# Graph layers on one core: the later layers spread over 29 slots, four graphs to a loop body

## The reference

```
hi = x @ W1[:H];  hj = x @ W1[H:]                       # block 0, for every pair (i, j) of nodes
y  = layernorm(relu(hi[i] + hj[j] + b1) @ W2 + b2) * gamma + beta
x  = layernorm(x + sum_j adj[i, j] * y[i, j])
x  = layernorm(x + relu((D^-1/2 adj D^-1/2 x) W^T + b))  # block 1
x  = layernorm(x + mask * (relu(((1 + eps) x + adj^T x) W1 + b1) W2 + b2))   # block 2
h  = x; three times: h = relu(layernorm(adj^T (h Ws[i]) + bs[i] + h) * g + beta)   # block 3
out = layernorm(x + h)
```

## Time and profile before

| what | value |
|---|---|
| median of 3 runs | 3404.64 us |
| profiled execution | 3402.17 us |
| its span | 3400.4 us |
| TensorE busy | 2933.5 us (86%) |
| VectorE busy | 2919.2 us (86%) |
| ScalarE busy | 2821.7 us (83%) |
| GpSimd busy | 403.7 us (12%) |
| mean granted TensorE clock | 0.945 |
| y products, L369 | 4096 instructions, 2152.3 us busy |
| weighted sums, L624 | 8192 instructions, 1953.1 us busy |
| hidden units on ScalarE, L507 | 1429.6 + 219.4 us busy |
| squares, L517 | 1024 instructions, 1164.1 us busy |

### The profile page before, as it was taken

How to read it: one execution, slowest core, us unless ns; L and a number is a source line. 1 busy time by engine, 2 the same in 40 slices (tenths; PEclk the granted TensorE clock), 3 DMA queues, 4 the chain that set the end, 5 groups by cost and what they waited for, 6 DMA issues and landing times.

```text
span 3400.4 us, 69689 instructions
## 1 busy us (share of the span) xinstructions
PE 2933.5 (86%) x10882; PEld 1150.1 (34%) x10882; DVE 2919.2 (86%) x21905; ACT 2821.7 (83%) x7620; POOL 403.7 (12%) x978
## 2 busy tenths in 40 slices
PE   8988888888888888888888888888888888888894
PEld 2333333333333333333333333333333333333332
DVE  5988888888888888888888888888888888888896
ACT  8988888888888888888888888888888888888892
POOL 0111111111111111111111111111111111111111
PEclk9999999999999999999999999999999999999996
DMA  3544444444444444444444344444444444434442
GB/s 123 208 159 174 182 167 156 169 191 162 158 171 183 169 156 159 196 167 158 158 181 184 156 159 185 179 159 157 175 190 156 159 175 183 164 156 167 192 162 106
DMA packets 170182, 570.56 MB, mean 168 GB/s; under 512 B 68608, under 2 KB 104320, under 8 KB 104320
## 3 DMA queue, kind: packets, MB, share of 16 engines
q1 hardware_dynamic: 169856, 567.82, 42.8%
HBM read 555.17 MB, written 8.39 MB: 166 GB/s over the span
## 4 chain that ended last, share of the span: by engine, by line
DVE 29%; PE 24%; issue 17%; ACT 14%; SPq 5%; DMA 5%; POOL 4%; DVEq 1%; ACTq 0%; POOLq 0%
PE y_ps L369 14%; DVE h L624 13%; ACT h L507 8%; PE ss_ps L381 6%; DVE h L610 5%; DMA devs<-dev_rows 5%; SPq L286 5%; POOL rs L850 3%; ACT sq L517 2%; DVE gT L624 2%; PE prod_bank L432 2%; ACT dev_rows L524 2%; DVE stats L648 2%; ACT h L555 1%; DVE x L657 1%
## 5 line engine op out<-in xcount | busy, mean ns | idle before, releaser
L369 PE MATMUL y_ps<-h,w2c 128*128 128x512 f32 x4096 | 2152.3, 637 | 209.7 <-DVE h L610 207.1
L624 DVE CUSTOM_DVE_ANT_0 h<-h,cb 128x128 f32<-128x128 f32 x8192 | 1953.1, 283 | 9.4 <-DMA cb<-c_scratch 0.4
L507 ACT ACTIVATE h<-uv_ps,uT 128x128 f32<-128x128 f32 x4928 | 1429.6, 400 | 235.5 <-DVE gT L624 230.3
L517 ACT ACTIVATE sq<-y_ps,b2c_col 128x1024 f32<-128x1024 f32 x1024 | 1164.1, 1137 | 143.8 <-PE y_ps L369 134.9
L369 PEld LDWEIGHTS y_ps<-h,w2c 128*128 128x128 f32 x4096 | 694.7, 196 | 1091.2 <-issue 934.0
L610 DVE TENSOR_SCALAR h<-vT,uT 128x128 f32<-128x128 f32 x2560 | 591.8, 282 | 188.6 <-issue 158.8
L624 DVE DVE_READ_ACCUMULATOR2_ANT gT<- 128x1 f32 x8192 | 670.8, 82 | 0.1
L381 PE MATMUL ss_ps<-sq,sel 128*32 128x512 f32 x4096 | 581.4, 642 | 0.5 <-ACT sq L517 0.5
L848 POOL TENSOR_TENSOR var_eps<-mv,eps_col 128x1 f32<-128x1 f32 x448 | 84.8, 189 | 2657.3 <-DVE mv L651 2657.3
L850 POOL TENSOR_TENSOR rs<-var_eps,minus_half 128x1 f32<-128x1 f32 x448 | 277.0, 618 | 35.1
L507 ACT ACTIVATE h<-vT,uT 128x128 f32<-128x128 f32 x704 | 219.4, 400 | 0.0
(11 more groups left out here) (99 smaller groups left out, 1556.2 us busy)
## 6 DMA issues: line engine op xcount, KB each, us to landing
cb<-c_scratch SPq DMA_DIRECT2D x512, 1024.0 KB, 8.1
adj_c<-in_adj_dram SPq DMA_DIRECT2D x512, 8.0 KB
devs<-dev_rows SPq DMA_DIRECT2D x512, 8.0 KB
x_in<-in_x_dram SPq DMA_DIRECT2D x64, 64.0 KB, 9.5
c_scratch<-c SPq DMA_DIRECT2D x128, 32.0 KB, 1.4
adj_in<-in_adj_dram SPq DMA_DIRECT2D x64, 64.0 KB, 2.0
x_res<-in_x_dram SPq DMA_DIRECT2D x64, 64.0 KB, 1.9
out_dram<-x SPq DMA_DIRECT2D x64, 64.0 KB, 10.1
```

Of the source, the lines that this page charges most:

```text
L369: op = pe.matmul(y_ps[:, t % 2, c0:c0 + COLS], w2c[:], h[:, t, c0:c0 + COLS], start=True, stop=True)
L507: op = act.activation(h[:, t, n * P:(n + 1) * P], v, ACT.Relu, bias=uT[:, i:i + 1])
L517: act.activation(sq[:, t % SQ_RING, :], y_ps[:, t % 2, :], ACT.Square, bias=b2c_col[:], scale=float(P) ** -0.5).then_inc(sq_done, 1)
L624: op = dve.tensor_tensor_reduce(h[:, t, cols], h[:, t, cols], cb[:, t // 2, c0:c0 + P], 1.0, 0.0, ALU.mult, ALU.add, gT[:, i:i + 1])
```

## The change

The later layers get a table of their own length, 29 slots, and start at lag 32 (28 after START), a whole number of iterations, so that in each iteration the graph two back is at slot s and the graph three back at slot s + 16. All buffers of the later layers get a second copy, picked by the parity b of the graph, and each parity has its own PSUM bank for prod, the turned adjacency and the coefficients' sum. uT and vT get a second copy too; turning x and making u and v are moved to slots 1 to 3 of the same graph. The weighted sums lag 14 slots behind START, not 15. VectorE makes two hidden units in each slot. A norm is applied seven places after its first step (before: four, and five for the affine of block 3). The loop body holds four graphs. SP loads for the later layers ahead of the output's store.

```
-TTR_LAG = START + 15
-TAIL_LAG = START + 29
+TTR_LAG = START + 14
+TAIL_LAG = START + 28
+UNROLL = 4
+SPLIT_AT = 13
-NORM_AT, AFFINE_AT = 4, 5
+NORM_AT = 7
-def vector_units(t):
-    return 3 if t % 2 == 0 else 2
+VECTOR_UNITS = 2
...
-    ("g_keep", 2, 0), ("l0_mm", 2, 2), ("l0_sum", 2, 5), ("ln0", 2, 6), ("x1_scaled", 3, 3),
-    ("l1_agg", 3, 4), ("l1_agg_keep", 3, 8), ("l1_mm", 4, 2), ("l1_bias", 4, 5), ("l1_relu", 4, 7),
-    ("ln1", 5, 0), ("l2_agg", 5, 4), ("l2_agg_keep", 5, 8),
...
-    ("l3_relu2", 14, 5), ("final_sum", 14, 7), ("ln3", 14, 8),
+    ("g_keep", 2, 0), ("l0_mm", 2, 4), ("l0_sum", 3, 3), ("ln0", 3, 4), ("x1_scaled", 4, 5),
+    ("l1_agg", 5, 0), ("l1_agg_keep", 5, 8), ("l1_mm", 6, 0), ("l1_bias", 6, 7), ("l1_relu", 7, 0),
+    ("ln1", 7, 2), ("l2_agg", 8, 4), ("l2_agg_keep", 9, 2),
+    ("l2_mm1", 9, 4), ("l2_relu", 10, 2), ("l2_mm2", 10, 4), ("l2_sum", 11, 2), ("ln2", 11, 3),
+    ("l3_agg0", 12, 4), ("l3_agg_keep0", 13, 2), ("l3_mm0", 13, 4), ("l3_sum0", 14, 2),
+    ("l3_ln0", 14, 3), ("l3_relu0", 16, 2), ("l3_agg1", 19, 0), ("l3_agg_keep1", 19, 8),
+    ("l3_mm1", 20, 0), ("l3_sum1", 21, 1), ("l3_ln1", 21, 2), ("l3_relu1", 22, 6),
+    ("l3_agg2", 23, 0), ("l3_agg_keep2", 23, 8), ("l3_mm2", 24, 0), ("l3_sum2", 25, 1), ("l3_ln2", 25, 2),
+    ("l3_relu2", 26, 6), ("final_sum", 28, 2), ("ln3", 28, 3),
...
-        prod = prod_bank[:, 0, :]
+        prod_bank = [ps(f"prod_bank{b}", [P, 4, P]) for b in range(2)]
+        xturn_ps, u_ps, v_ps = (uv_ps[:, i, :] for i in range(3))
+        prod = [prod_bank[b][:, 0, :] for b in range(2)]
...
-            for i in range(4):
-                iteration(i + 1, (i, *(i - d if i >= d else None for d in range(1, 4))))
-            with eng.Fori(4, G - 1) as g:
-                iteration(g + 1, (g, g - 1, g - 2, g - 3))
+            first = 4 + (G - 5) % UNROLL
+            for i in range(first):
+                iteration(i + 1, about(i), i % 2)
+            with eng.Fori(0, (G - 1 - first) // UNROLL) as rounds:
+                for n in range(UNROLL):
+                    g = UNROLL * rounds + (first + n)
+                    iteration(g + 1, (g, g - 1, g - 2, g - 3), (first + n) % 2)
...
+        def tails(graphs, buf, s):
+            return [(graphs[d], (buf - d) % 2, (s + SLOTS * (d - 2)) * FINE) for d in (2, 3)]
...
+                    load_tail(old, 1 - buf)                      # SP, now here
+                if oldest is not None:
+                    wait_apart(sp, normed["ln3"], oldest + 1)
...
-                if old is not None:
-                    load_tail(old)                               # SP, was last
...
-                    hidden_step = BLOCK_UNITS if ht == 0 else 0
+                    hidden_step = BLOCK_UNITS if ht == 0 else 0 if t == 0 else 1
...
-                        later_layers(g, place * FINE + k, place * FINE + k + 1)
+                        for g, b, place in tails(graphs, buf, s):
+                            later_layers(g, b, place + k, place + k + 1)
```

More of the change, by code:

```diff
@@ L406, in later_layers @@
                     wait(pe, g_kept, g + 1)
[L407 to L410, removed]
+                    pe.matmul(out, gT_keep[:, b, :], w2cg[:], start=True, stop=False)
+                    pe.matmul(out, adjT[:, b, :], beta0[:], start=False, stop=True).then_inc(l0_made, 1)
                 if due("l1_agg"):
@@ L453, in _ @@
             pe.wait_ge(ident_set, 1)
-            turn_x(0)
             pe.wait_ge(weights_in, 16 * WEIGHTS)
@@ L459, in _, with iteration @@
             pe.wait_ge(set_up, 1)
-            def iteration(after, graphs):
+            def iteration(after, graphs, buf):
                 new = graphs[0]
@@ L465, in iteration @@
                         later_set_up()
-                    g, place = lagging(graphs, s, TAIL_LAG)
                     yg, t = lagging(graphs, s, START + 1)
-                    if s == START - 1 and new is not None:
-                        make_uv(new)
                     if yg is not None:
                         products(yg, t, 0)
-                    if s == 14 and after is not None:
-                        turn_x(after)
-                    later_layers(g, place * FINE, place * FINE + 4)
+                    for g, b, place in tails(graphs, buf, s):
+                        later_layers(g, b, place, place + 4)
                     if yg is not None:
                         products(yg, t, 1)
-                    later_layers(g, place * FINE + 4, (place + 1) * FINE)
+                    for g, b, place in tails(graphs, buf, s):
+                        later_layers(g, b, place + 4, place + FINE)
+                    if s == 1 and new is not None:
+                        turn_x(new)
+                    if s == 2 and new is not None:
+                        make_uv(new)
                     sg, t = lagging(graphs, s, START + 3)
@@ L582, in iteration @@
                         deviations(vg, t // HALF)
-                    later_layers(g, place + 1, place + 4)
-                    first = vector_units(ht)
-                    for n in range(first, DUO_UNITS):
-                        if n == first + 2:
-                            later_layers(g, place + 4, place + 6)
-                        if n == first + 4:
-                            later_layers(g, place + 6, place + 8)
-                        if hg is not None:
-                            hidden(hg, ht, n)
-                    if s == SLOTS - 1 and after is not None:
-                        keep_xT(after)
-                    if s == START - 1 and new is not None:
-                        keep_uv(new)
-                    later_layers(g, place + 8, place + FINE)
+                    if s == START - 1 and new is not None:
+                        keep_uv(new, buf)
+                    tail_steps(1, 4)
+                    for n in range(VECTOR_UNITS, DUO_UNITS):
+                        if n == VECTOR_UNITS + 2:
+                            tail_steps(4, 6)
+                        if n == VECTOR_UNITS + 4:
+                            tail_steps(6, 8)
+                        if hg is not None:
+                            hidden(hg, hb, ht, n)
+                    if s == 1 and new is not None:
+                        keep_xT(new)
+                    tail_steps(8, FINE)
             program(act, iteration)
@@ L601, in _, with hidden @@
         def _(dve):
-            def hidden(g, t, n):
+            def hidden(g, b, t, n):
                 if n == 0:
```

259 lines of the change are left out of this document (130 added, 129 removed), and 5 rows, old and new, of the table AT.

## The result

The changed kernel takes 3016.64 us in the median (3013.08 to 3017.53, four runs) against 3405.36 us for the kernel before timed beside it: ratio 0.8855, 95% interval 0.884 to 0.887. The forecast was 3089 us with a range from 3020 to 3200; the time lies 3.4 us under its lower end. The direction and the two mechanisms came out, the size of the largest term, the period, did not. The profiled execution has a span of 3014.8 us.

The account below looks back on a forecast made before the run. No single engine was taken to bound the kernel, but work order and hand-overs. Start 185, 59 periods of 46.3 (2731.7), branches back 44.2 and end 124.2 gave 3085 us; plus 1.8 and 2.5, 3089 us, range 3020 to 3200.

Parts of the forecast that it names:

- the two mechanisms: Of the 315 us forecast gain, 153 from fewer branches back and some 160 from a shorter period per graph.
- the period: Time per graph inside the loop: 49.07 us falls to 46.3, ScalarE's busy time; floor 45.1 (VectorE), ceiling 47.5.
- The branches back: End of each loop pass: 13 instead of 58, at 3.4 us each, 153 us less; 44 us remain.
- The third rival: VectorE's floor is reached in the loop: period 45.1 us, 3018 us or less; chance 0.16.
- VectorE's waits: Later layers' wider places remove VectorE's 1.4 us for GpSimd power and 1.0 us for TensorE's products per graph.
- The lag: Weighted sums 14 slots behind: ScalarE's 1.0 us wait goes; coefficients lose one slot, with 1.4 us to spare.
- The slower rival: Coefficients reach VectorE's weighted sums too late: up to 7.0 us wait per graph, 3502 us; chance 0.03.
- SP's queue, turn_x and keep_uv: Reordered SP transfers: no gain, no loss; turn_x and keep_uv moved to slots 1 to 3, costed at zero.
- The ends: Outside the steady periods: 185 us up to iteration 4's gT_keep, 124.2 us from iteration 63's copy to the end.
- the drain's 5 us: Last graph's later layers share queues with the graph before: between 0 and 14 us more, taken as 5.
- The first rival: ScalarE takes over and its waits for y_ps and aggregates stay: period 48.7 us, 3231 us; chance 0.11.
- the second: Rival: the loop's stall is per graph, not per branch back, so 45 x 3.4 us returns, 3242 us; chance 0.03.

Follow-up runs that it names:

- experiment 1: The kernel before with only its loop body changed to four graphs (13 branches back, not 58): 3264.16 us, ratio 0.9597.
- experiment 7: The changed kernel with ScalarE reading v from SBUF in all slots (SPLIT_AT 0, not 13): 3167.66 us, ratio 0.9318.
- experiment 4: The changed kernel with VectorE making three and two hidden units in turn, as before the change: 3047.04 us, ratio 0.8961.
- experiment 5: The changed kernel with three and two VectorE units in turn, plus 100 filler memsets shifting the loop in VectorE's stream: 3022.88 us, ratio 0.8876.
- experiment 8: The changed kernel, two runs: ScalarE squaring only half of each y_ps tile, 2949.68 us; VectorE without three of eight units' weighted sums, 3003.89 us.
- experiment 10: The changed kernel with norms applied four places after their first step, not seven: 3117.1 us, ratio 0.9158.
- experiment 9: The changed kernel with weighted sums lagging 15 slots again, not 14: 3107.32 us; with block 3's first relu one slot later, 3041.97 us.
- the third run of experiment 11: The changed kernel with fourteen graphs to a body and VectorE making three units in every fourth slot, lag 14: 2948.09 us, ratio 0.8661.

## Why the prediction was right and wrong

*The branches back.* Right in kind and number: 13 issue waits of 35.9/13 = 2.8 us. The 3.4 us for one was too low already for the kernel before (3.9, experiment 1), since the pass taken as free of a branch back still held part of its catching up; in the new kernel it is 5.2, which makes 68 us where the sum had 44. It cannot be read off another kernel: it runs from 3.6 us (experiment 7) to 9.3 (experiment 4). One cause is shown, a second stall that depends on where the loop begins in the instruction stream (experiments 4 and 5); what the catching up costs in each kernel is not explained.

*The period.* This step failed: "I take 46.3 us, ScalarE's busy time". The period measured 44.85 us; 59 x 1.45 = 86 us. That ScalarE becomes the bound was right (experiments 7 and 8), and that three loaded engines don't reach the floor was wrong: the period is ScalarE's own floor (44.86 us in experiment 8), with nothing added for handing over. Busy time is the union of spans, and a span's end overlaps the next start only when the engine is dense. Before, ScalarE had several pauses a graph: in the period of the earlier trace rows its 120 activations take 42.3 us from start to start at their usual distances, where the busy time is 44.33. So adding 2.0 us to the old busy time counted the ends of spans ahead of pauses too. The prediction had the better measure next to it, 43.4 us from start to start, and rejected it. That measure in turn is 1.45 us too small, for two reasons. The 18 hidden units of the last three slots read v from SBUF at 0.29 us instead of 0.25 (0.75 us; before the change it was two slots, SPLIT_AT makes it three). And the starts of units that read PSUM run ahead of the work, by 0.8 us a graph (last section). The 13 smaller ones, estimated at 0.2 each, measure 2.4 us together and not 2.6; some 0.1 us stays unexplained. The third rival named 3018 us, and by VectorE's floor of 45.1; the number fits, the engine does not.

*VectorE's waits.* That the wider places remove 1.4 and 1.0 us was right in the changed kernel, and experiment 10 shows that it mattered more than the sum gave it (1.9 us a graph for three places). The forecast subtracted them on VectorE, and then set the period by ScalarE regardless.

*The lag.* "One slot less to arrive, 1.4 us to spare" was too kind: VectorE waits for cb 114 times, 0.95 us each. With the old lag (experiment 9) these waits are gone and the time is not shorter, so they cost nothing that shows. The slower rival's mechanism was there, with a quarter of its wait (108 against 59 x 7.0 = 413 us) and none of its price.

*SP's queue, turn_x and keep_uv.* No visible cost inside a body; at each branch back ScalarE waits 3.6 us for x turned (47.1/13), since TensorE waits for VectorE there.

*The ends.* Iteration 4's copy was forecast at 185 and is at 184.96. From iteration 63's copy on it takes 3014.8 - 2898.85 = 116.0 us, not 124.2: the drain's 5 us were not needed, and 3.2 more were saved. From the last copy to the end it is 32.8 us, as before.

*The sum.* -86 for the period, +24 for the branches, -8 for the rest: 3085 less 70 = 3015. The first rival (3231) and the second (3242) are out: ScalarE's wait for y_ps fell from 134.9 to 6.9 us, and the stalls are per branch back.

## What to carry to other kernels

To forecast a period after waits are removed, take the engine that will be densest and count its work from start to start, in a dense stretch and with each operand's memory; the busy time of an engine that pauses is too large for it (46.3 us for 44.85 here). Starts alone can be a little short, where spans grow from one to the next (0.8 us here). Read the cost of a loop's branch back from the distance of the same landmark with and without it, in the kernel that will run and not from the pass right behind a branch back, and expect it to vary with body length and position: long bodies pay up to a point (13 to 3 branches 1.1%, 3 to 1 nothing). In a statically ordered pipeline each step needs slack behind the engine it waits for, above all ahead of the saturated engine: a relu one place behind its affine, not ten, cost 65 us here, three places for the norms 100 us.

## What the runs showed of the hardware

ScalarE takes 1.75 us for six 128 x 128 activations from start to start where the input is in SBUF and 1.50 where it is in PSUM, though both show spans of 400 ns when the engine has pauses. With all hidden units reading from SBUF the period rose by 2.5 us (experiment 7).

A dense ScalarE whose hidden units read PSUM shows spans that grow while the starts keep their distance. Squares of its timeline in the changed kernel: one after a pause of 0.9 us, three slots on and six slots on, then one three more slots on, whose hidden units read SBUF:

```profile
1638.05 1.11 ACT L522 ACTIVATE sq<-y_ps,b2c_col 128x1024 f32<-128x1024 f32 x1
...
1645.69 1.30 ACT L522 ACTIVATE sq<-y_ps,b2c_col 128x1024 f32<-128x1024 f32 x1
...
1653.99 1.49 ACT L522 ACTIVATE sq<-y_ps,b2c_col 128x1024 f32<-128x1024 f32 x1
...
1662.96 1.49 ACT L522 ACTIVATE sq<-y_ps,b2c_col 128x1024 f32<-128x1024 f32 x1
```

The same square takes 1.11 us and then 1.49, some 0.06 more with each slot that reads PSUM; over the three slots that read SBUF it stays at 1.49. In experiment 7, where all slots read SBUF, it hardly grows (0.005 us a slot). Two squares of its timeline, twelve slots apart:

```profile
1502.78 1.11 ACT L522 ACTIVATE sq<-y_ps,b2c_col 128x1024 f32<-128x1024 f32 x1
...
1538.19 1.12 ACT L522 ACTIVATE sq<-y_ps,b2c_col 128x1024 f32<-128x1024 f32 x1
```

So I take it that where hidden units read PSUM the work falls behind its starts, by 13 x 0.06 = 0.8 us a graph, and the periods bear it out. From start to start ScalarE's 127 activations of a graph take 43.9 us in the changed kernel, and 43.9 + 0.8 = 44.7 us is nearly its period of 44.85. In experiment 7 the count from start to start is 47.2 us with nothing to add, and the period is 47.3: 78 x 0.04 = 3.2 us more from start to start, less the 0.8, is the 2.5 us measured.

What has fallen behind is made up where a start comes late, and the profile shows no idle time for it. In the middle of the window with ScalarE at 45.23 of 45.23 us VectorE, which had just waited 1.38 us for cb, finishes an affine at 1542.81 us; the relu that needs it starts 0.03 us later, some 0.9 us behind its turn, and has a short span again:

```profile
1542.46 0.35 DVE L738 SCALAR_TENSOR_TENSOR z_aff<-z_aff,rs,l3beta 128x128 f32<-128x128 f32 x1
```

```profile
1540.99 1.88 ACT L512 ACTIVATE h<-uv_ps,uT 128x128 f32<-128x128 f32 x4
1542.84 0.31 ACT L560 ACTIVATE h<-z_aff 128x128 f32<-128x128 f32 x1
```

So ScalarE at 100% is not proof that it never waits. That such short waits cost nothing here is what experiment 8 says: with over a fifth of VectorE's work gone the mean period is the same (44.88 us).

A branch back stalls VectorE 2.8 us (3.1 us with two graphs to a body, 4.0 us in the third run of experiment 11), and a second time by 1.9 to 2.2 us in three of the loops; 100 filler instructions ahead of one of these loops removed the second stall.
